# A graph layer with a mixture of experts on one core: residual sum moved into DRAM, weight splitting moved two steps earlier, expert stage written out

## The reference

```
x = x + gnn(layernorm(x))
    h = silu(x W_in^T + b_in)
    term = h; out = h
    for i in 1..6: term = A term / i ; out = out + term      # A: mean over incoming edges
    result = out W_out^T + b_out
x = x + ffn(layernorm(x))
    xn = layernorm(x)*gamma + beta; logits = xn Wr + br; the two best of 8 experts, softmax weights
    y += w_e * (gelu(xn W1[e] + b1[e]) W2[e] + b2[e])
```

## Time and profile before

| what | us |
|---|---|
| median of 3 runs | 1402.74 (1402.63 to 1402.93) |
| the profiled execution, its own time | 1399.97 |
| its span, first to last instruction | 1398.2 |
| steps 3 and 4 | 599 to 873.7 |
| last step, from tile 5 on | 909 to 1075 |
| expert stage, PE | 1130.5 to 1357 |
| PE busy, share of the span | 1199.9 (86%) |
| DVE busy, share of the span | 744.3 (53%) |

### The profile page before, as it was taken

How to read it: one execution, slowest core, us unless ns; L and a number is a source line. 1 busy time by engine, 2 the same in 40 slices (tenths; PEclk the granted TensorE clock), 3 DMA queues, 4 the chain that set the end, 5 groups by cost and what they waited for, 6 DMA issues and landing times.

```text
span 1398.2 us, 28001 instructions
## 1 busy us (share of the span) xinstructions
PE 1199.9 (86%) x7796; PEld 836.1 (60%) x7797; DVE 744.3 (53%) x1521; ACT 364.5 (26%) x706; POOL 167.7 (12%) x193
## 2 busy tenths in 40 slices
PE   4896999999999999999999999988885468778860
PEld 2784776665666666666666665545453357667750
DVE  7588999963333333333333333366566744554445
ACT  0574656640000000000000000022213223433423
POOL 2000000000000000000000000111111134555440
PEclk8897999999999999999999999999987579989995
DMA  5110010022111111111101110233332012112119
GB/s 155 30 52 19 23 38 29 29 84 57 41 44 37 38 40 45 33 35 44 46 27 45 41 46 22 51 106 102 101 109 76 17 50 65 62 61 64 58 45 269
DMA packets 65272, 81.72 MB, mean 58 GB/s; under 512 B 10997, under 2 KB 55981, under 8 KB 65085
## 3 DMA queue, kind: packets, MB, share of 16 engines
q1 hardware_dynamic: 49126, 49.55, 12.4%
q10 hardware_dynamic: 9908, 16.37, 4.2%
q0 software_dynamic: 6176, 15.01, 3.5%
HBM read 62.34 MB, written 19.50 MB: 59 GB/s over the span
## 4 chain that ended last, share of the span: by engine, by line
PE 63%; DVE 11%; DMA 9%; issue 8%; DVEq 3%; ACT 2%; POOL 1%; another core or an unknown queue 1%; ACTq 1%; SPq 0%; POOLq 0%
PE ps L1552 39%; PE ps L1530 7%; PE ps L1498 4%; PE ps L1658 3%; PE ps L1675 3%; DVE v_b L986 2%; DMA adj<-L_ffn_W 2%; DMA v_b<-xs_dram,v_a 2%; PE ps L1466 2%; DMA adj<-y_dram 2%; PE ps L1598 2%; PE ps L1477 1%; DMA v_a<-x 1%; DVEq L375 1%
## 5 line engine op out<-in xcount | busy, mean ns | idle before, releaser
L1552 PE MATMUL ps<-v_a,adj 125*125 125x512 f16 x1375 | 297.3, 379 | 0.0
L1552 PE MATMUL ps<-v_b,adj 125*125 125x512 f16 x1250 | 270.2, 379 | 2.2 <-DVE v_b L1011 2.2
L1552 PEld LDWEIGHTS ps<-v_a,adj 125*125 (+1 forms) x1375 | 187.6, 136 | 109.0
L1552 PEld LDWEIGHTS ps<-v_b,adj 125*125 x1250 | 170.6, 136 | 101.6 <-issue 2.6
L993 DVE SCALAR_TENSOR_TENSOR t_hi<-ps,cinv,t_hi 125x256 f32<-125x256 f32 x125 | 60.3, 482 | 284.2 <-ACT t_hi L750 284.2
L750 ACT ACTIVATE t_hi<-ps,cinv 125x256 f32<-125x256 f32 x125 | 59.4, 475 | 526.0 <-PE ps L1552 496.3
L986 DVE TENSOR_TENSOR v_b<-v_b 125x2560 f16<-125x2560 f16 x125 | 180.3, 1485 | 7.1 <-PE ps L1498 6.5
L1598 PE MATMUL ps<-v_b,adj 125*125 125x512 f16 x625 | 153.6, 409 | 5.5 <-DVEq L1128 3.4
L1675 PE MATMUL ps<-adj,v_b 128*128 x672 | 115.3, 283 | 25.5 <-issue 19.0
L727 ACT ACTIVATE adj<-ps 125x625 f32 (+1 forms) x125 | 111.8, 906 | 75.1 <-PE ps L1498 74.3
L1598 PEld LDWEIGHTS ps<-v_b,adj 125*125 (+1 forms) x625 | 90.5, 147 | 61.5 <-issue 13.1
(11 more groups left out here) (230 smaller groups left out, 940.1 us busy)
## 6 DMA issues: line engine op xcount, KB each, us to landing
h_ring<-h_dram SPq DMA_DIRECT2D x150, 125.0 KB
w_piece<-L_ffn_W SPq DMA_DIRECT2D x64, 128.0 KB, 2.1
adj<-L_ffn_W ACTq DMA_DIRECT2D x16, 512.0 KB, 6.1
v_a<-x SPq DMA_DIRECT2D x25, 125.0 KB
xs_dram<-v_a SPq DMA_DIRECT2D x25, 125.0 KB
adj<-x ACTq DMA_DIRECT2D x5, 560.0 KB
adj<-y_dram SPq DMA_DIRECT2D x5, 560.0 KB
adj<-y_dram ACTq DMA_DIRECT2D x5, 560.0 KB
```

The source lines that it names most:

```text
L1552: last = te.matmul(ps[0:NP, u, :], of_tile(adj[0:NP, 0:ADJ], i, u, a * NP, NP), source[:, a, :], start=(a == 0), stop=(a == T - 1))
```

## The change

1. **h + x + b_out in DRAM.** POOL issues, after the weight maxima of step 2, three transfers one after the other over all 3125 rows: `hx_dram` is copied from `h_dram`, then x is added by an accumulating transfer, then b_out. The last step loads `hx_dram` in place of `h_dram`, and one DVE instruction writes x1 directly. The load of x, POOL's L637, DVE's L1189 and the buffers `vfin` and `x_i` go. SP waits for the third transfer at the start of the last step.
2. **Weights.** Steps 1 and 2 now load all weights once, in 32 pieces of 256 KB, for the maxima; the scales are worked out at the start of step 3. Steps 3 and 4 load each piece again, ACT writes the high part, DVE the low part, and SP stores both to `w16_dram`. The buffers lie in the last tiles of the term that is being written. In the last step SP loads the finished parts, 512 KB for each expert and layer; ACT's L797 and DVE's L1230 go, and so does ACT's wait for the weights.
3. **Expert stage without a loop.** All 56 tiles are written out. Each engine loads the table entry of the next tile in every tile: PE one value (`part_of`, which serves both layers), DVE two, ACT one. The weight regions are numbered so that one entry is enough. The waits then have constant values.

```diff
@@ sync, steps
+                if s > 0:
+                    sp.wait_ge(S["tile_ps"], s * T)
+                def store(i, u):
+                    sp.wait_ge(S["piece_used"], (s - 1) * NE // 2 * WP + i * WP + (u + 3))
+                    sp.dma_start(w16_half(s, i, u, 0), w_hi16[:, :]).then_inc(S["w16_out"], 16)
+                    sp.dma_start(w16_half(s, i, u, 1), lo16).then_inc(S["w16_out"], 16)
@@ sync, last step
+            sp.wait_ge(S["hx_ok"], 48)
-                                 h_v[:, bass.ds(m, 1), :].rearrange("p a f -> p (a f)")).then_inc(h_in[u % 2], 16)
-                    need(sp, S["x1_ok"], m - 1)
-                    sp.dma_start(x_i[ring(0, u)], x_v[:, bass.ds(m, 1), :].rearrange("p a f -> p (a f)")).then_inc(xi_in[ring(0, u)], 16)
+                                 hx_v[:, bass.ds(m, 1), :].rearrange("p a f -> p (a f)")).then_inc(h_in[u % 2], 16)
+                if has_unit(i, u):
+                    e, layer = (u - 1) // 2, (u - 1) % 2
+                    part = bass.ds(WIN * i - WIN + PARTS_W[e][layer], 1)
+                    if u == 1:
+                        sp.wait_ge(S["tile_ps"], LAST + 5 * i)
...
+                    sp.dma_start(w_both(part), w16_v[bass.ds(2 * i - 2 + e, 1), layer:layer + 1, :, :, :].rearrange("a b k n w -> k (a b n w)")
+                                 ).then_inc(S["w_in"], 16)
@@ gpsimd
+            pool.wait_ge(S["w_top_ok"], 1)
+            g.partition_all_reduce(w_all, w_top, 128, bass.bass_isa.ReduceOp.max).then_inc(S["w_all_ok"], 1)
...
+            g.dma_start(hx_dram, h_dram).then_inc(S["hx_ok"], 16)
+            pool.wait_ge(S["hx_ok"], 16)
+            g.dma_start(hx_dram, x, max_dma_last_dim=8192, accum_op=ALU.add).then_inc(S["hx_ok"], 16)
+            pool.wait_ge(S["hx_ok"], 32)
+            g.dma_start(hx_dram, bass.AP(b_out.tensor, 0, [[0, N], [1, D]]), accum_op=ALU.add).then_inc(S["hx_ok"], 16)
-                if has(0):
-                    pool.wait_ge(xi_in[ring(0, u)], 16 * (uses(i, u, 0) + 1))
-                    g.tensor_tensor(x_i[ring(0, u)], x_i[ring(0, u)], bo_bc[0:NP, :], ALU.add).then_inc(S["xb_ok"], 1)
@@ scalar, steps 3 and 4
+                            act.wait_ge(piece_in[u % 2], 16 * ((s - 1) * NE + (u // 2 + 1)) + 32 * i)
+                            act.wait_ge(S["w16_out"], 32 * (i * WP + u + 1) + 32 * NE * 2 * (s - 3))
+                            a.activation(w_hi16[:, :], raw[u % 2], ACT.Copy,
+                                         scale=sw[:, bass.ds((s - 3) * NE + 2 * i + u // 2, 1)]).then_inc(S["piece_hi"], 1)
@@ vector, steps
+                            if s <= 2:
+                                dve.wait_ge(piece_in[u % 2], 16 * ((s - 1) * NE + (u // 2 + 1)) + 32 * i)
+                                v.tensor_reduce(w_max[:, bass.ds(count, 1)], raw[u % 2], AX.X, ALU.max,
+                                                apply_absolute_value=True).then_inc(S["piece_used"], 1)
+                            else:
+                                dve.wait_ge(S["piece_hi"], count - NE * 2 * 2 + 1)
+                                v.scalar_tensor_tensor(lo16, raw[u % 2], sw[:, bass.ds((s - 3) * NE + 2 * i + u // 2, 1)],
+                                                       w_hi16[:, :], ALU.mult, ALU.subtract).then_inc(S["piece_used"], 1)
@@ vector, last step
-                    dve.wait_ge(S["xb_ok"], m)
-                    v.scalar_tensor_tensor(xt, vfin[ring(1, u)], scale[0:NP, 1:2], x_i[ring(1, u)], ALU.mult, ALU.add).then_inc(S["x1_ok"], 1)
-                    v.drain()
-                if has_unit(i, u):
...
-                    v.scalar_tensor_tensor(w_part(part, 1), w_raw32(bass.ds(WIN * i - WIN + PART_RAW[layer], 1)),
-                                           sw[:, bass.ds(layer * NE + 2 * i - 2 + e, 1)], w_part(part, 0),
-                                           ALU.mult, ALU.subtract).then_inc(S["w_lo"], 1)
-                    v.scalar_tensor_tensor(vfin[RB[u]], h_ring[0:NP, u % 2, :], scale[0:NP, 0:1], t_hi[0:NP, :],
-                                           ALU.mult, ALU.add).then_inc(S["h_used"], 1)
+                    v.scalar_tensor_tensor(x1[:, bass.ds(m, 1), :].rearrange("p a f -> p (a f)"), t_hi[0:NP, :], scale[0:NP, 1:2],
+                                           h_ring[0:NP, u % 2, :], ALU.mult, ALU.add).then_inc(S["h_used"], 1)
@@ expert stage
+def ffn_tiles(eng, count, unroll, lag, tables, steps, transposed, hidden, result):
+    entries = {0: [load(0, eng) for load in tables]}
+    transposed(0)
+    transposed(1)
+    for j in range(count + lag):
+        for b in range(steps):
+            if j >= lag:
+                result(j - lag, b, *entries[j - lag], alone=j >= count)
+            if b == 0 and j + 2 < count:
+                transposed(j + 2)
+            if j < count:
+                hidden(j, b, *entries[j])
+            if b == 0 and j + 1 < count:
+                entries[j + 1] = [load(j + 1, eng) for load in tables]
+        entries.pop(j - lag, None)
```

More of the change, by code:

```diff
@@ L272, in gnn_ffn @@
         idx_g, idx_s = fa(FT, I32), fa(FT, I32)
[L275 to L278, removed]
+        exp_of, part_of = (over(adj, ((T - 1) * REG + XW) * 2 + 4 * D * FR + n * 4 * FT, FT, I32)
+                                      for n in range(2))
         xn2 = [fa(D, F32, NP) for _ in range(3)]
@@ L343, in gnn_ffn @@
         xs_out = [sem(f"xs_out{r}") for r in range(3)]
[L344 to L345 removed]
+        piece_in = [sem(f"piece_in{r}") for r in range(2)]
         g_in = [sem(f"g_in{r}") for r in range(FU)]
@@ L856, in tile @@
                 last.then_inc(S["gelu_ok"], 1)
-            def group(i):
-                es = experts(i, act, 0, FU)
-                for u in range(FU):
-                    tile(i, u, es[u])
-            group(0)
-            with act.Fori(1, FT // FU) as i:
-                group(i)
+            e = experts(0, act)
+            for j in range(FT):
+                e_next = experts(j + 1, act) if j + 1 < FT else None
+                tile(j, e)
+                e = e_next
             for r in range(FR):
@@ L1662, in hidden, with result @@
                     last.then_inc(S["ffn_h"], 1)
-            def result(i, u, b, part2, alone=False):
-                j = FU * i + u
-                r = u % 2
+            def result(j, b, part, alone):
+                u, r = j % FU, j % 2
                 if b == 0 and alone:
@@ L1679, in result @@
                     last.then_inc(S["ffn_y"], 1)
-            ffn_tiles(pe, FT, FU, LAG, (parts1,), (parts2,), HK, transposed, hidden, result)
-def ffn_tiles(eng, count, unroll, lag, hidden_tables, result_tables, steps, transposed, hidden, result):
-    groups = count // unroll
-    def entries(tables, i, first, tiles):
-        return list(zip(*(load(i, eng, first, tiles) for load in tables)))
-    def group(i, first, last):
-        now, before = entries(hidden_tables, i, 0, unroll), entries(result_tables, i, -lag, unroll)
-        for u in range(unroll):
-            for b in range(steps):
-                if not (first and u < lag):
-                    result(i + (u - lag) // unroll, (u - lag) % unroll, b, *before[u])
-                if b == 0 and not (last and u >= unroll - 2):
-                    transposed(i + (u + 2) // unroll, (u + 2) % unroll)
-                hidden(i, u, b, *now[u])
-        if last:
-            for u, values in enumerate(entries(result_tables, groups, -lag, lag)):
-                for b in range(steps):
-                    result(i, unroll - lag + u, b, *values, alone=True)
-    transposed(0, 0)
-    transposed(0, 1)
-    group(0, True, False)
-    with eng.Fori(1, groups - 1) as i:
-        group(i, False, False)
-    group(groups - 1, False, True)
+            ffn_tiles(pe, FT, FU, LAG, (parts,), HK, transposed, hidden, result)
+def ffn_tiles(eng, count, unroll, lag, tables, steps, transposed, hidden, result):
[13 more added lines that the diff above has]
+        entries.pop(j - lag, None)
 def newton(v, r, var, tmp):
```

239 lines of the change are left out of this document (121 added, 118 removed).

## The result

| | before | after |
|---|---|---|
| median of the runs, us | 1402.68 (4 runs, 1401.05 to 1402.93) | 1384.17 (4 runs, 1382.16 to 1387.56) |
| profiled execution: time, span | 1399.97, 1398.2 | 1384.08, 1382.2 |
| ratio after to before | | 0.987, 95% interval 0.985 to 0.989 |

The kernel is 18.5 us faster. The forecast was 1356, 47 us faster: the sign was right, the size was off by 28 us, though the time lies inside the range of 1334 to 1391.

A forecast was written before the change was run, and what follows sets the result against it. PE was taken to bound steps 3 and 4, a chain through several engines the last step, loop-head loads much of the expert stage's loss. Terms: -30 + 1 + 0 - 18 = -47 us on 1399.97, 1353; as median 1356, range 1334 to 1391.

The forecast's parts named there:

- h + x + b_out: Three DRAM transfers after step 2: 60 us in all, 272 us available, so they end in time at cost 0.
- the +1 of steps 1 to 4: Steps 1 to 4: added splitting on DVE and ACT hidden under PE; from 0 to 4 x 1.0, taken as +1 us.
- (a): Rival: the expert stage gives nothing, a tile takes 4.06 us as before; total 1374, chance 0.22.
- (b): Rival: in the expert stage DVE's second load is dear, 4.4 us a tile; total 1391, chance 0.10.
- (d): Rival: the sum in DRAM is late, each us past 873.7 adds one to the total; chance 0.07.
- if steps 3 and 4 grow: Sign against the prediction: steps 3 and 4, expected still at 5.4 us a tile, get longer.
- The last step: Last step: weight waits, L1189 and L1230 go; 28.0 us saved over 19 intervals, -30 us in sum.
- 6.08: Last step, body with u > 0: 6.65 us less 0.57 for L1189 gives 6.08 us.
- 9.25: Last step, body with u = 0: 9.82 us less 0.57 gives 9.25 us.
- a bound of 31 us: Last step: most that the 19 intervals can save, if PE sets the pace at 6.4 us each.
- The expert stage: Expert stage: loop heads go, one PE load a tile at 0.50 us; tile 4.06 to 3.70 us, -18 us.
- (c): Rival: both stages at their good bounds, last step 31 + 2, expert tile 3.37 us; total 1337, chance 0.11.

The follow-up runs named there:

- e1: Changed kernel without the three transfers of POOL; last step loads h alone, x and b_out missing from the output: 1349.86 us, ratio 0.957.
- e2: Changed kernel without the third transfer only (b_out missing from the output), copy of h and adding of x kept: 1348.69 us, ratio 0.957.
- e5: Changed kernel with the same three transfers issued before step 1, from about 300 us on, instead of after step 2: 1365.91 us, ratio 0.991.
- e11: From e1: in place of the three sums, seven plain copies of h to DRAM on POOL's queue: 1390.12 us in one execution.
- e12: From e1: the same seven plain copies of h as in e11, but issued on ACT's queue: 1395.29 us in one execution.
- e6: Changed kernel with each transfer cut in 25 parts of 125 rows, released by PE's tile count in steps 3 and 4: 1325.63 us, ratio 0.962.
- e8: From e1: x and b_out added in the last step as before the change, weights still split in steps 3 and 4: 1345.68 us, ratio 0.977.
- e9_paced_again: The kernel of e6 run once more on another chip, against the kernel before: 1347.38 us, ratio 0.957.

## Why the prediction was off

**The step that failed** is "I take that they end in time, and their cost is 0", of h + x + b_out, with the +1 of steps 1 to 4, which priced only the engines' part of those steps. In time they were: 97 us in a stretch of 272. The price was not lateness but company. I asked of the transfers only when they end, not what else uses the DMA engines while they run. The h loads, one each 5.4 us, and the pieces feed DVE and ACT, and ACT waits for the stores of the split weights; from 606 to 704 DVE fell 59 us behind by them, of which 18.6 are hidden, and step 3 grew by 40.8 us. e1 and e2 show that the transfers are the cause, e5, e11 and e12 that place, kind and queue don't matter, e6 that cutting and spacing them removes the cost. On the profiled run the forecast was 1353; with 40.8 in place of the +1 it would have been 1393, and the rest came 9 better, which makes the 1384. That the time lies inside the range is luck: its upper part was there for rivals (a) and (b), and neither came.

Rival (d) named "h loads in between", but as something that delays the sum. It is the other way round: the sum delays the h loads and the stores. The last line on what would make the prediction fall ("if steps 3 and 4 grow") named the place.

**The last step**, -30 forecast, -35.1 measured. Right was that the waits for weights go. The u > 0 bodies behind tile 10 take 6.0 us (forecast 6.08) and the u = 0 bodies 9.0 (9.25), but the 6.0 agree by luck. I got 6.08 by taking 0.57 off a chain through DVE, POOL and ACT; what sets the pace now is PE, which has no gap between 990 and 1020. Its large groups start 5.99 us apart:
```profile
990.00:1020.00 30.00, 30.00 (x156) 20.09 (x155) 15.25 (x50) 4.77 (x13) 3.26 (x4) 1.00 0.42 120
```
```profile
998.55 5.59 PE L1633 MATMUL ps<-v_b,adj 125*125 125x512 f16 x25
...
1004.54 5.59 PE L1633 MATMUL ps<-v_b,adj 125*125 125x512 f16 x25
```
I had added PE's three groups to 6.4 us, though they overlap, and so set a bound of 31 us on the saving of the 19 intervals, which measured 33.8. The rest of the surplus is in the first four of the sixteen u > 0 bodies: they take 4.95 to 5.31 us, 3.9 us less together than the 6.08 that I took for all. Removing L1189 was priced at its own 0.57 us a tile; in e8 the whole hand over through POOL and DVE costs 1.04.

**The expert stage**, -18 forecast, -21.4 measured: a tile of 3.63 for 3.70. Two errors cancel in part: the load takes 0.30, not 0.50, and something like 0.1 more than I left for gathers and the like remains. The 3.63 belong to this chip; on that of e5, e6 and e8 the same stage runs at 3.31 to 3.33. Of the rivals, (a) didn't come (the stage gained), (b) neither (DVE's two loads take 0.3 us each), and (c) came in the last step, past its bound of 31 + 2, and was then swallowed by step 3.

**The time without the stall.** e6_paced and e9_paced_again are what the forecast described: -53.3 and -58.2 us against the kernel before on their chips, for -47.

## What to carry to other kernels

A background transfer costs in two ways: it may be late, and it may hold the DMA engines against small loads that an engine consumes every few us. For the second ask how long the longest piece in one go is, and compare it with the slack (here some 18 us) of whoever waits for small transfers, stores included; the average DMA share (0.14 in steps 3 and 4 before) says nothing on it. If it doesn't fit, cut the transfer in parts that a consumer's progress counter releases: here the same bytes then cost nothing in steps 3 and 4. A second `w_hi` buffer, which would take ACT's wait for the stores out of the way, was not tried.

## What the runs showed of the hardware that was not expected

- 3.2 MB copied inside DRAM took 12.9 us; adding 3.2 MB took 20.8 us in packets of 8000 B, and adding one 1 KB row 3125 times took 63.3 us, in packets of 0.229 us each, over three times as long for the same bytes.
- Loads of 125 and 256 KB beside such a transfer took 28 and 29 us, and a store of 128 KB beside seven copies 67 (e11) and 63 (e12), although they stood on another queue.
- In straight code a load of one value into an engine's register took 0.30 us and one of eight 0.60; in the loop of the kernel before the loads of eight took up to 2.17 us.
- The same kernel differs between chips by up to 2.3% (1378.95 to 1410.73 us for the kernel before). e6_paced and e9_paced_again, the same kernel, are equal up to the last step (1042.3 and 1041.7 us at tile 24); a tile of the expert stage takes 3.33 and 3.70 us. There DVE stands before its results for something that the trace calls remote in the second only, in windows of 160 us, e6_paced first:
```profile
L1458 DVE SCALAR_TENSOR_TENSOR adj<-ps,v_a,adj 128x256 f32<-128x256 f32 x46 | 22.3, 484 | 15.0 <-issue 12.1 <-PE ps L1715 2.9
```
```profile
L1458 DVE SCALAR_TENSOR_TENSOR adj<-ps,v_a,adj 128x256 f32<-128x256 f32 x41 | 19.8, 484 | 35.1 <-remote 24.3 <-issue 7.8 <-PE ps L1715 3.0
```
By the code the other thing that DVE waits for there is the scatter of an earlier tile. That the scatters are slower on that chip was not measured by itself.
